# A GRU scan with routed low-rank experts: the reset gate and the candidate's state part get PSUM banks of their own, and their seeds move in ScalarE's order

## The reference

```
gi = x_t @ W_ih + b_ih ; gh = h @ W_hh + b_hh
r = sigmoid(i_r + h_r) ; z = sigmoid(i_z + h_z)
n = tanh(i_n + r * h_n)
h = (1 - z) * n + z * h
...
combine = top-2 of softmax(h/|h| @ router_w), made to sum to 1
out = x + sum_e combine[e] * (h @ Wa[e] @ Wb[e])
```

## Time and profile before

| | |
|---|---|
| median of 3 runs | 1042.89 us (1042.72 to 1044.01) |
| span of the profiled execution | 1040.8 us |
| PE busy | 1011.4 us (97%) |
| PEld busy | 828.4 us (80%) |
| DVE busy | 860.0 us (83%) |
| ACT busy | 722.6 us (69%) |
| POOL busy | 299.0 us (29%) |
| matmuls | 28409 |

### The profile page before, as it was taken

One profiled execution on the slowest core, in us unless ns is written; L12 is line 12 of the kernel. 1 busy time (PEld: TensorE's weight loads), 2 busy tenths in 40 slices (PEclk: granted clock), 3 DMA queues, 4 the chain that ended last, 5 costly groups with the idle time before them and its releaser, 6 DMA issues.

```text
span 1040.8 us, 67010 instructions
## 1 busy us (share of the span) xinstructions
PE 1011.4 (97%) x28409; PEld 828.4 (80%) x28409; DVE 860.0 (83%) x3215; ACT 722.6 (69%) x2824; POOL 299.0 (29%) x762
## 2 busy tenths in 40 slices
PE   5789999999999999999999999999999999999997
PEld 3677888888888888888888888888888888888875
DVE  6889888888888888888888888888888888888886
ACT  7687666767666767667767667667766767766663
POOL 2032232322233332233332233332233332223223
PEclk9999999999999999999999999999999999999999
DMA  8230111111111111111111111111111011110001
GB/s 295 84 94 17 30 32 29 30 27 30 29 32 29 29 27 30 29 32 30 29 28 28 29 32 32 27 30 27 29 32 32 26 30 28 29 32 20 9 9 33
DMA packets 49522, 39.24 MB, mean 38 GB/s; under 512 B 34676, under 2 KB 39112, under 8 KB 49224
## 3 DMA queue, kind: packets, MB, share of 16 engines
q1 hardware_dynamic: 48376, 31.41, 11.1%
q10 hardware_dynamic: 848, 3.54, 1.0%
HBM read 18.94 MB, written 8.39 MB: 26 GB/s over the span
## 4 chain that ended last, share of the span: by engine, by line
PE 91%; DVE 5%; ACT 2%; DMA 1%; issue 1%; POOL 0%; ACTq 0%; DVEq 0%; POOLq 0%
PE ybank L1014 18%; PE pairs L883 17%; PE obank L1037 15%; PE gates L958 11%; PE gates L963 10%; PE nbank L912 7%; PE zbank L973 5%; PE zbank L969 5%; DVE tr L762 1%; PE nbank L994 1%; DMA wih<-in_L_cond_W_ih 1%; DVE pre L765 1%; DVE acc L815 1%; ACT nn L624 1%; DVE pre L771 1%
## 5 line engine op out<-in xcount | busy, mean ns | idle before, releaser
L883 PEld LDWEIGHTS pairs<-wx,xs 128*32 128x32 f16 x6144 | 140.7, 96 | 105.8 <-issue 101.7
L883 PE MATMUL pairs<-wx,xs 128*32 128x256 f16 x6144 | 215.6, 275 | 0.0
L1014 PE MATMUL ybank<-hparts,wa 128*128 128x128 f16 x3024 | 212.5, 220 | 0.0
L458 POOL TENSOR_TENSOR y<-y 128x128 f16<-128x128 f32 x256 | 111.7, 436 | 348.1 <-ACT y L658 190.0
L1037 PE MATMUL obank<-wb,y 128*128 128x512 f16 x738 | 199.3, 379 | 0.0
L1014 PEld LDWEIGHTS ybank<-hparts,wa 128*128 128x128 f16 x3024 | 169.8, 98 | 26.9
L762 DVE STREAM_TRANSPOSE tr<-gates 128x256 f32<-128x256 f32 x256 | 115.1, 450 | 72.4 <-PE gates L963 68.5
L616 ACT ACTIVATE rr<-pre 128x64 f32<-128x64 f32 x256 | 65.7, 257 | 155.6 <-DVE pre L765 155.2
L958 PE MATMUL gates<-whh,st 128*32 128x256 f16 x4080 | 155.8, 273 | 11.3 <-DVE st L788 10.8
L963 PE MATMUL gates<-whh,hparts 128*32 128x256 f16 x4080 | 155.9, 273 | 0.0
L815 DVE SCALAR_TENSOR_TENSOR acc<-obank,comb,acc 128x512 f32<-128x512 f32 x184 | 136.9, 744 | 0.2
(11 more groups left out here) (134 smaller groups left out, 1701.4 us busy)
## 6 DMA issues: line engine op xcount, KB each, us to landing
out<-outb SPq DMA_DIRECT2D x63, 128.0 KB
xin<-in_x SPq DMA_DIRECT2D x58, 128.0 KB
wih<-in_L_cond_W_ih ACTq DMA_DIRECT2D x4, 768.0 KB, 7.7
whh<-in_L_cond_W_hh SPq DMA_DIRECT2D x4, 768.0 KB, 11.8
wih<-in_L_ffn_Wb SPq DMA_DIRECT2D x8, 256.0 KB, 2.7
xs<-xh SPq DMA_TRANSPOSE x116, 2.8
wih<-in_L_ffn_Wa SPq DMA_DIRECT2D x4, 256.0 KB, 4.2
whh<-in_L_ffn_Wa SPq DMA_DIRECT2D x4, 256.0 KB, 2.6
```

Of the source, the lines that this page charges most:

```text
L458: nc.gpsimd.tensor_tensor(y[:, m % YB, 1, :], y32[:, :], y[:, m % YB, 0, :], ALU.subtract).then_inc(ylo_ready, 1)
L883: mm = nc.tensor.matmul(bank[32 * j:32 * j + 32, P:3 * P], turned(b, k, ph)[:, t0:t0 + 2 * B], wx[:, pw, k, j, :], start=False, stop=(k == ...
L1014: mm = nc.tensor.matmul(y_at(m)[:, 0:P], wa[:, pw, k, e, :], hparts[:, f % HB, k, :, ph * B:(ph + 1) * B], start=(n == 0), stop=(n == 3 * ...
```

## The change

The two `gates` banks are one tile `rh` of two banks: bank `HN` (0) holds the candidate's state part, bank `RG` (1) the reset gate, each in columns 0 to 127, and both are used in every step. `state_part` does 128-column matmuls: low part for r (the loop names RG first), low part for the candidate, then the high part for r with `r_done` behind it, and the high part for the candidate with `hn_done`. DVE turns r's bank, turns the candidate's, adds r's halves, adds the candidate's, and goes on with z as before; the product waits for `hn_summed` beside `r_ready`. ACT issues `seed(n + 1)` right behind the sigmoid of r of step n, as one instruction over both banks, and no longer in `beside(n)`.

```diff
-        gates = [ps(f"gates{i}", [P, 4 * P]) for i in range(2)]
+        rh = ps("rh", [P, 2, 4 * P])
+        gates = [rh[:, i, :] for i in range(2)]
...
-                wait(act, rh_turned, n - 1)
-                if n == 1:
+                wait(act, hn_turned, n)
+                if n == 0:
 
                     act.wait_ge(gi_ready, 1)
-                nc.scalar.activation(gates[n % 2][:, 0:2 * P], pairs[n // 2 % 2][:, 0:2 * P], ACT.Copy,
-                                     scale=step_rows[:, q:q + 1]).then_inc(seeded, 1)
+                nc.scalar.activation(rh[:, :, 0:P], pairs[n // 2 % 2][:, 0:2 * P].rearrange("p (g c) -> p g c", g=2),
+                                     ACT.Copy, scale=step_rows[:, q:q + 1]).then_inc(seeded, 1)
...
             def gru_step(n):
-                act.wait_ge(rh_summed, n + 1)
+                act.wait_ge(r_summed, n + 1)
                 nc.scalar.activation(rr[:, :], pre[:, RG, :, :].rearrange("p k b -> p (k b)"), ACT.Sigmoid,
                                      scale=1 / PROD_SCALE).then_inc(r_ready, 1)
+                if n + 1 < T:
+                    seed(n + 1)
...
-                if n + 2 < T:
-                    seed(n + 2)
...
-            seed(1)
...
-                g = gates[n % 2]
-                dve.wait_ge(rh_done, n + 1)
-                nc.vector.transpose(tr[:, 0:2 * K, :].rearrange("p (g k) c -> p g k c", k=K),
-                                    g[:, 0:2 * P].rearrange("p (g c k) -> p g k c", g=2, k=K)).then_inc(rh_turned, 1)
-                dve.wait_ge(rh_turned, n + 1)
-                nc.vector.tensor_tensor(pre[:, 0:2, :, :].rearrange("p g k b -> p (g k) b"), tr[:, 0:2 * K, 0:B],
-                                        tr[:, 0:2 * K, B:2 * B], ALU.add).then_inc(rh_summed, 1)
+                dve.wait_ge(r_done, n + 1)
+                nc.vector.transpose(tr[:, RG * K:(RG + 1) * K, :], gates[RG][:, 0:P].rearrange("p (c k) -> p k c", k=K)
+                                    ).then_inc(r_turned, 1)
+                dve.wait_ge(hn_done, n + 1)
+                nc.vector.transpose(tr[:, HN * K:(HN + 1) * K, :], gates[HN][:, 0:P].rearrange("p (c k) -> p k c", k=K)
+                                    ).then_inc(hn_turned, 1)
+                dve.wait_ge(r_turned, n + 1)
+                nc.vector.tensor_tensor(pre[:, RG, :, :], tr[:, RG * K:(RG + 1) * K, 0:B],
+                                        tr[:, RG * K:(RG + 1) * K, B:2 * B], ALU.add).then_inc(r_summed, 1)
+                dve.wait_ge(hn_turned, n + 1)
+                nc.vector.tensor_tensor(pre[:, HN, :, :], tr[:, HN * K:(HN + 1) * K, 0:B],
+                                        tr[:, HN * K:(HN + 1) * K, B:2 * B], ALU.add).then_inc(hn_summed, 1)
...
+                dve.wait_ge(hn_summed, n + 1)
                 dve.wait_ge(r_ready, n + 1)
...
-                for k in range(K):
-                    for j in range(K):
-                        nc.tensor.matmul(g[32 * j:32 * j + 32, 0:2 * P], st[:, k, :], whh[:, 1, k, j, 0:2 * P],
-                                         start=False, stop=False, skip_group_check=True)
+                for g in (RG, HN):
+                    for k in range(K):
+                        for j in range(K):
+                            nc.tensor.matmul(gates[g][32 * j:32 * j + 32, 0:P], st[:, k, :],
+                                             whh[:, 1, k, j, g * P:(g + 1) * P], start=False, stop=False,
+                                             skip_group_check=True)
                 pe.wait_ge(both_parts_ready, 2 * (n + 1))
-                for k in range(K):
-                    for j in range(K):
-                        mm = nc.tensor.matmul(g[32 * j:32 * j + 32, 0:2 * P], prior[:, k, :], whh[:, 0, k, j, 0:2 * P],
-                                              start=False, stop=(k == K - 1), skip_group_check=True)
-                mm.then_inc(rh_done, 1)
+                for g, done in ((RG, r_done), (HN, hn_done)):
+                    for k in range(K):
+                        for j in range(K):
+                            mm = nc.tensor.matmul(gates[g][32 * j:32 * j + 32, 0:P], prior[:, k, :],
+                                                  whh[:, 0, k, j, g * P:(g + 1) * P], start=False, stop=(k == K - 1),
+                                                  skip_group_check=True)
+                    mm.then_inc(done, 1)
```

More of the change, by code:

```diff
@@ L155, in gru_moe_kernel @@
         last_y, last_o = [zbank, ybank], pairs + [obank] + gates
+        FROM_PAIRS, FROM_GATES = (0, 1), (3, 4)
         first_banks = [obank, ybank, obank]
         def n_at(b, m):
-            return (gates[1], zbank, nbank, obank)[m] if b == 0 else nbank
+            return (gates[HN], zbank, nbank, obank)[m] if b == 0 else nbank
         def y_at(m):
@@ L200, in gru_moe_kernel @@
         z_seeded = sem("z_seeded")
-        rh_done = sem("rh_done")
+        r_done = sem("r_done")
+        hn_done = sem("hn_done")
         z_done = sem("z_done")
-        rh_turned = sem("rh_turned")
-        rh_summed = sem("rh_summed")
+        r_turned = sem("r_turned")
+        hn_turned = sem("hn_turned")
+        r_summed = sem("r_summed")
+        hn_summed = sem("hn_summed")
         z_turned = sem("z_turned")
@@ L935, in first_state_part @@
                 pe.wait_ge(both_parts_ready, 2)
-                sides = ((gates[0], slice(0, 2 * P), rh_done), (zbank, slice(2 * P, 3 * P), z_done))
+                sides = ((gates[RG], slice(P, 2 * P), r_done), (gates[HN], slice(0, P), hn_done),
+                         (zbank, slice(2 * P, 3 * P), z_done))
                 for pw in range(2):
@@ L944, in first_state_part @@
                             for j in range(K):
-                                mm = nc.tensor.matmul(bank[32 * j:32 * j + 32, 0:cols.stop - cols.start],
+                                mm = nc.tensor.matmul(bank[32 * j:32 * j + 32, 0:P],
                                                       (st if pw else prior)[:, k, :], whh[:, pw, k, j, cols],
@@ L1023, in expert_up @@
                     wait(pe, acc_done, m)
-                elif o_at(m) is obank and m < LEFT + len(last_o):
-                    pe.wait_ge(acc_done, LEFT)
-                elif o_at(m) in pairs and m < LEFT + len(last_o):
+                elif m - LEFT in FROM_PAIRS:
                     pe.wait_ge(seeded, T)
                     pe.wait_ge(z_seeded, T)
-                elif o_at(m) in gates and m < LEFT + len(last_o):
-                    pe.wait_ge(rh_turned, T)
+                elif m - LEFT in FROM_GATES:
+                    pe.wait_ge(hn_turned, T)
+                elif m - LEFT < len(last_o):
+                    pe.wait_ge(acc_done, LEFT)
                 else:
@@ L1072, in _ @@
             zeros = st[:, :, :].rearrange("p k c -> p (k c)")
-            for g, n_cols in ((gates[0], 2), (gates[1], 2), (zbank, 1)):
-                for c in range(n_cols):
-                    mm = nc.tensor.matmul(g[:, c * P:(c + 1) * P], zeros, zeros, start=(c == 0), stop=(c == n_cols - 1),
-                                          skip_group_check=True)
-                mm.then_inc(primed, 1)
+            for g in (gates[HN], gates[RG], zbank):
+                nc.tensor.matmul(g[:, 0:P], zeros, zeros, start=True, stop=True, skip_group_check=True
+                                 ).then_inc(primed, 1)
             pe.wait_ge(ident_step, 2)
```

## The result

The changed kernel takes **1169.34 us** (median of 4 runs, 1167.83 to 1176.37) where the kernel before takes 1043.08 (4 runs, 1042.72 to 1044.01). The ratio is 1.1224, with a 95% interval of 1.1193 to 1.1255. I had forecast 1044.8 us with a range from 1043.0 to 1047.5, so the forecast is wrong by more than a hundred microseconds, far outside its range. The likeliest "slower" case, 1046.6 us, is as wrong.

A forecast was written before the change was run, and what follows sets the result against it. PE's column stream was taken to bound 230 middle steps and the scan both ends. PE's +4.6 us and the scan's -2.7 us gave +1.9 us on 1042.89, so 1044.8 us, range 1043.0 to 1047.5.

The forecast's parts named there:

- The likeliest "slower" case: Scan steps at both ends: gain falls to about 0.05 us a step while PE's price comes; 1046.6 us, chance 0.44.
- PE's stream gets longer: State products on PE: sixteen narrow quads for eight wide add 20 ns in each of 230 steps, +4.6 us.
- nothing there is waited for: The 230 steps that PE bounds: PE has no waits, so the added 20 ns a step comes out in full.
- PE's issue becomes the limit: Rival on PE: 32 added matmuls with loads take 27 ns each, 0.88 us a step; 1245 us, chance 0.01.
- A middle step of 3.87 us: Sign in the changed trace: a step in the middle takes 3.87 us where it took 3.85.
- Narrow matmuls in place of the wide ones: Sign in PE's state products: two groups of 16 narrow matmuls where a wide group was.
- The scan's step: Sign at both ends: a step takes 3.55 to 3.56 us, with step 5's product 2.13 us behind PE's start.
- The rival of the held-up sum and the second wait: DVE in scan steps: candidate's turn delays r's sum and the added wait delays the product; gain about 0.05 us, chance 0.44.
- The distance from the new state to PE's start: Sign in middle steps: the time from new state to PE's next start grows from 0.29 to about 0.46 us.
- The turn in step 18: Sign near the start: r's turn stands where the turn of both was, 1.59 us behind PE's start, DVE being late.
- PE waits for nothing between 108 and 990 us: Middle of the run: PE waits for nothing; any wait there was named as showing the forecast wrong.
- the scan's gain: Scan-bound steps at both ends: 0.155 us saved in each of 16, smaller changes in others, -2.7 us in all.

The follow-up runs named there:

- the series: Kernel before with a quarter, half or all of the reset-gate and candidate state matmuls cut to 128 columns: 1046.8, 1060.1 and 1168.8 us, against 1043 uncut.
- the pair with fewer instructions: Kernel before and changed kernel, both with expert first products, gate input products and z's state products in fewer, wider matmuls of equal columns: 1033.56 and 1037.81 us.
- the third experiment: Changed kernel with the experts' first products and the gates' input products in fewer, wider matmuls of equal columns: 1072.93 us, ratio 1.0269 to the kernel before.

## Why the prediction was wrong, step by step

**The step that failed** is the last sentence of "PE's stream gets longer": "Weight loads double too, but line 969 already runs with one load for each 128 columns, 16 in 0.22 us, so they fit beside." It is true of the row that it rests on, since loads and narrow matmuls do run at 14 ns each in the changed kernel too. But it costs a stream by its rate over 16 instructions, and what limits a long stream is the supply of instructions over 256. With it fell "nothing there is waited for", the sentence under which 230 steps were multiplied by 20 ns alone. That term, +4.6 us, was right; the waits that stood beside it at nothing took 113.3 - 4.5 = 109 us in the 227 middle steps, because a block of 256 instructions held 3.46 us of work and took 4.0 to come. The change adds 64 instructions to a step of 226, and I had counted them only as columns.

The sign that I missed stood in the kernel's own page: a queue named "instruction" whose packets times 256 are PE's instructions, with 4.41 us between them, and in the trace a room of 1.3 us (2.7 - 1.4). The added instructions take 4.41 - 3.46 = 0.95 us of it. That would have been a warning and not yet the loss: the rest of the room went because the transfers also began later in the changed kernel (1.3 us behind the entry for 0.5). I had a rival for much slower, "PE's issue becomes the limit", at 0.01. Its 1245 us came from a price for each added instruction, and the series refutes that form of it. Its plain statement was right. What I should have asked is not how fast PE can take one instruction but how fast the next hundreds arrive.

The Trainium skill, "Runtime: NRT & Kernel Launch", section "Instruction fetch mechanics", says that instructions come in blocks of 16 KiB, 256 of them, fetched while the current block runs, and that the cost of a border is mostly hidden. The traces agree on the size, on the fetch beside the work, and on the cost for the kernel before. They disagree for the changed one: 4.0 us for a block against 3.46 us of work, 120 pauses at one place modulo 256. The section also gives PE room for 2048 instructions, and a little further on calls the memory only two lines of 16 KiB. PE here behaves like the second: at none of the 226 and 290 entries into a block in the traces of the two kernels had a later block landed yet.

**What held.** Point by point, against "What would show it":
- *A middle step of 3.87 us.* The steps without a pause take it, 20 ns more than before. In the pair with fewer instructions the same difference stands in every step (3.827 - 3.807), and 227 steps are longer by 879.4 - 874.9 = 4.5 us: my term of +4.6 us for 230.
- *Narrow matmuls in place of the wide ones.* They are there in the listed order, 32 at 507.05 and 32 at 507.50, where 16 and 16 were.
- *The scan's step.* In step 5 of the changed kernel a pause stands inside z's products, and the step takes 3.95 us. So here is step 2, which has none, with DVE and ACT up to the product:

```profile
34.48 0.63 PE L969 MATMUL rh<-whh,st 128*32 128x128 f16 x32
...
35.38 0.32 DVE L765 STREAM_TRANSPOSE tr<-rh 128x128 f32<-128x128 f32 x1
...
35.62 0.30 DVE L768 STREAM_TRANSPOSE tr<-rh 128x128 f32<-128x128 f32 x1
35.85 0.18 DVE L771 TENSOR_TENSOR pre<-tr 128x64 f32<-128x64 f32 x1
...
36.07 0.26 ACT L621 ACTIVATE rr<-pre 128x64 f32<-128x64 f32 x1 [0.67 <-DVE pre L771]
36.10 0.31 DVE L777 STREAM_TRANSPOSE tr<-zbank 128x128 f32<-128x128 f32 x1
36.23 0.43 ACT L583 ACTIVATE rh<-pairs,step_rows 128x256 f32<-128x256 f32 x1
...
36.45 0.23 DVE L780 TENSOR_TENSOR pre<-tr 128x64 f32<-128x64 f32 x1
36.59 0.22 DVE L784 TENSOR_TENSOR rhn<-rr,pre 128x64 f32<-128x64 f32 x1
```

  Behind PE's start the turn of r stands at 0.90 us (forecast 0.91), the candidate's at 1.14 (1.13), r's sum at 1.37 (1.36), the sigmoid at 1.59 (1.62), the product at 2.11 (2.13). The step is 3.534 us, where before it was 3.71: a gain of 0.18 us where I had 0.155. The rival of the held-up sum and the second wait, 0.05 us, is refuted: z's turn starts 0.25 us behind r's sum, and the product follows z's sum after 0.14, as before.
- *The distance from the new state to PE's start.* I had 0.46 us for the middle, up from 0.29. In the 25 of these steps that have no pause its median is 0.49, and in the changed kernel with fewer instructions 0.45 (0.25 in its partner).
- *The turn in step 18.* I had it where it was, 1.59 us behind PE's start, because DVE is late there. It stands at 1.23 in the changed kernel, where PE is late as well, but at 1.60 in the changed kernel with fewer instructions, as forecast.
- *PE waits for nothing between 108 and 990 us:* wrong, and this was named as the sign of a wrong forecast.

**A second, smaller miss.** Of the scan's gain I had expected 2.7 us. In the pair with fewer instructions, which is the best case for it, steps 1 to 18 cost 70.76 us against 69.66, and steps 248 to 254 cost 25.66 against 26.45. So 0.8 us are gained at the end, and at the start 1.1 are lost where I had a gain. Single steps there still have the full gain (3.534), but others take 4.25, 4.12 and 4.70 us, with the "issue" waits listed above. The DMA engines are at work on the late weights at that time, but whether these delay the blocks, or the narrow steps at the start, which have no expert matmuls to stretch a block, wasn't separated. In the changed kernel itself it costs more: the first 18 steps lose 6.0 us. The offset: +4.5 in the middle, +1.1 and -0.8 at the ends, -0.3 at the start and behind the last step make the pair's +4.6 us of span.

So the forecast's picture of the engines was right to some hundredths of a microsecond a step, and its time wrong by 124 us, because one resource, the supply of instructions, was not in the picture. Taking the pair for the change without that resource, it would have come to 1043.1 + 4.3 = 1047.4 us: slower even so, by the miss at the start, and at the upper end of my range.

## What to carry to other kernels

Before you cut matmuls into smaller ones, count PE's instructions (loads too) and divide the time of a stretch by its number of 256-instruction blocks: here the kernel is safe at 4.4 us a block, loses 0.4% at 4.1, 1.7% at 3.9 and 12% at 3.5. An engine that is 97% busy without waits can be half a microsecond a block away from that edge (4.4 against 3.9), and the page shows it in the packets of the instruction queue. The number depends on the kernel: at 4.0 us a block the third experiment lost 2.7%, and two thirds of its pauses stood behind single blocks of 5.4 to 6.3 us. "Issue" idle time of PE in the midst of an accumulation, at distances of 256 instructions, is the mark; wider matmuls anywhere in the program cure it, not only where it was made worse.

## What was not expected of the hardware

- In the changed kernel a late block of 256 PE instructions takes 4.0 us (3.7 to 4.3) from the entry into the one before it to its use, of which only 1.1 us (0.88 to 1.4) is the 16 KB transfer: some 1.3 us pass before it and 1.4 us behind it. It hardly matters to it whether other queues move 27 or 5 GB/s.
- The part before the transfer varies most: 0.5 us (median) in the kernel before, 1.3 in the changed one, and 2.7 to 3.8 at twelve borders of the third experiment. The part behind it stays at 1.2 to 1.7 us at the borders where PE pauses.
- Matmuls of 8 columns, with a load each, still cost 0.25/32 = 8 ns apiece, four column tiles side by side; ones of 128 columns cost 14 ns. So with hardly any columns to stream the price of a matmul falls by less than half.
